# A fused cross-attention and expert block: weighted sums moved in front of the remainders and the scores in 41 of 64 steps

## The reference

```
q = layernorm(x) @ Wq;  k = ctx @ Wk;  v = ctx @ Wv
probs = softmax(q k^T / 8)          (per batch and head, 128 x 128)
x = x + tanh(g_xattn) * ((probs @ v) @ Wo + bo)
```

```
de = tokens scattered to the experts' slots by (top-2 choice, rank in arrival order)
eo = relu(de @ fc1^T + b1) @ fc2 + b2
x = x + tanh(g_ffn) * sum over the 2 choices of gate * eo
```

## Time and profile before

| | |
|---|---|
| median of 3 runs | 995.57 us (991.43 to 996.29) |
| the profiled execution | 994.87 us, span 993.1 us |
| TensorE busy | 949.4 us, 96% |
| VectorE busy | 676.3 us, 68% |
| ScalarE busy | 508.1 us, 51% |
| GpSimd busy | 281.8 us, 28% |
| mean granted clock of TensorE | 0.983 |

### The profile page before, as it was taken

How to read it: one execution, slowest core, us unless ns; L and a number is a source line. 1 busy time by engine, 2 the same in 40 slices (tenths; PEclk the granted TensorE clock), 3 DMA queues, 4 the chain that set the end, 5 groups by cost and what they waited for, 6 DMA issues and landing times.

```text
span 993.1 us, 18998 instructions
## 1 busy us (share of the span) xinstructions
PE 949.4 (96%) x7199; PEld 823.4 (83%) x7199; DVE 676.3 (68%) x1542; ACT 508.1 (51%) x1573; POOL 281.8 (28%) x293
## 2 busy tenths in 40 slices
PE   7799999999999999999999888999999999999996
PEld 5587877888878878878888786999999999999995
DVE  5768687686785886886776862757575665657572
ACT  3567376465664773673754621535444343435352
POOL 6803025024033043042041133222222223232222
PEclk8989999999999999999999998999999999999998
DMA  9096003011020021021011015254342435252521
GB/s 259 22 298 194 22 2 107 23 41 67 22 86 24 22 92 38 2 86 44 1 44 44 13 52 187 66 117 101 76 128 50 128 49 130 49 130 56 141 53 22
DMA packets 63099, 76.63 MB, mean 77 GB/s; under 512 B 6033, under 2 KB 55096, under 8 KB 63008
## 3 DMA queue, kind: packets, MB, share of 16 engines
q1 hardware_dynamic: 50720, 59.18, 20.0%
q0 software_dynamic: 12288, 16.23, 9.0%
HBM read 46.52 MB, written 29.49 MB: 77 GB/s over the span
## 4 chain that ended last, share of the span: by engine, by line
PE 73%; ACT 11%; DVE 8%; POOL 3%; DMA 2%; issue 2%; SPq 1%; POOLq 0%; DVEq 0%; another core or an unknown queue 0%
PE down L1211 6%; PE down L1210 6%; PE down L1209 6%; PE up L1195 6%; PE up L1196 6%; PE up L1197 6%; PE score L545 4%; ACT probs_odd L733 4%; ACT work L733 4%; PE out_bank L533 4%; PE probT L520 4%; DVE negmax L913 2%; PE rT L1179 2%; PE query_bank L466 2%; PE query_bank L464 2%
## 5 line engine op out<-in xcount | busy, mean ns | idle before, releaser
L1151 POOL DMA_INDIRECT out_dram<-eo,index x64 | 99.4, 1553 | 282.2 <-ACT eo L1253 250.4
L1245 ACT ACTIVATE hid<-up,b 128x512 f32<-128x512 f32 x128 | 88.3, 690 | 84.8 <-PE up L1197 84.8
L733 ACT ACTIVATE probs_odd<-score,negmax 128x128 f32<-128x128 f32 x256 | 91.3, 382 | 44.6 <-DVE negmax L913 44.6
L733 ACT ACTIVATE work<-score,negmax 128x128 f32<-128x128 f32 x256 | 91.4, 383 | 42.8 <-DVE negmax L913 42.8
L407 POOL DMA_INDIRECT disp<-packed,slots x64 | 68.8, 1075 | 133.8 <-DVE slots L904 92.4
L913 DVE TENSOR_REDUCE negmax<-score 128x4 f32<-128x512 f32 x128 | 82.0, 682 | 28.1 <-PE score L545 27.7
L698 ACT ACTIVATE k_sb<-key_bank 128x512 f32<-128x512 f32 x64 | 38.8, 606 | 112.8 <-PE key_bank L489 111.5
L1253 ACT ACTIVATE eo<-eo_raw,gate 128x256 f32<-128x256 f32 x64 | 30.9, 506 | 122.4 <-DVE eo_raw L1315 122.4
L1306 DVE TENSOR_TENSOR hid_l<-hid,hid_h 128x512 fp32r<-128x512 f32 x128 | 88.6, 693 | 4.4
L921 DVE COPY pT<-probT 128x512 f32<-128x512 f32 x128 | 82.2, 682 | 8.7 <-PE probT L520 7.4
L1315 DVE TENSOR_TENSOR eo_raw<-down,b 128x256 f32<-128x256 f32 x64 | 25.8, 423 | 86.4 <-PE down L1211 86.4
(11 more groups left out here) (253 smaller groups left out, 2788.8 us busy)
## 6 DMA issues: line engine op xcount, KB each, us to landing
rows<-disp SPq DMA_DIRECT2D x18, 516.0 KB, 5.4
w_raw<-fc1T_dram SPq DMA_DIRECT2D x9, 1024.0 KB, 8.3
w_raw<-fc_dram SPq DMA_DIRECT2D x9, 1024.0 KB, 10.9
disp<-fixed SPq DMA_DIRECT2D x1, 8256.0 KB, 33.8
rows<-x_dram SPq DMA_DIRECT2D x16, 512.0 KB, 4.3
out_dram<-rows SPq DMA_DIRECT2D x8, 512.0 KB, 3.1
c_raw<-ctxT_dram SPq DMA_DIRECT2D x8, 256.0 KB
c_raw<-ctxT_dram SPq DMA_DIRECT2D x16, 128.0 KB
```

The lines of the kernel that those rows point to most:

```text
L733: last = nc.scalar.activation(probs[w % 2][:, c, :], score[hh][:, b * P:(b + 1) * P], ACT.Exp, bias=negmax[:, w % 2, c:c + 1], accum_out=s ...
L1151: pool.indirect_dma_start(out=out_rows[:, :], out_offset=bass.IndirectOffsetOnAxis(ap=index[half][:, i:i + 1], axis=0), in_=eo[half][:, i, ...
L1245: nc.scalar.activation(hid[m % 2][:, :], up[m % 2][:, :], ACT.Relu, bias=b1[par][:, m:m + 1]).then_inc(s_hid, 1)
```

## The change

In steps without a second extra piece, TensorE's weighted sums and their wait for out_bank are issued behind V's main products (and behind the one extra piece, where there is one), in front of the two remainders and the scores. In steps with a second extra piece the order is as before.

```
             if kinds[1:]:
                 pe.wait_ge(s_at_split, w)
                 misc(kinds[1], out_bank, u // NP)
+            if w >= 0 and not kinds[1:]:
+                pe.wait_ge(s_at_split, w)
+                weigh_values(w)
             if u + 1 < STEPS:
                 keys_rest(u + 1)
             if i < STEPS:
                 values_rest(value_bank, i)
             scores(u)
-            if w >= 0:
-                if kinds[1:]:
-                    pe.wait_ge(*misc_done(kinds[1], u // NP))
-                else:
-                    pe.wait_ge(s_at_split, w)
+            if w >= 0 and kinds[1:]:
+                pe.wait_ge(*misc_done(kinds[1], u // NP))
                 weigh_values(w)
```

## The result

The changed kernel takes 1017.95 us (median of 6 runs, 1015.63 to 1021.03), the kernel before 994.83 (6 runs, 991.43 to 997.3): ratio 1.0229, 95% interval 1.0208 to 1.025. The direction was as predicted, the size not: 9.3 us were forecast, 23 came, and the time lies over the range. The profiled execution (1021.03 us, span 1019.2) is the slowest of the six, 26.1 over that of before.

The account below looks back on a forecast made before the run. TensorE's own work and the loop from one step's scores to the next q_sb were taken as nearly level bounds. Terms 7.4, 1.0, 0.9 and 0 made 9.3 us; 994.87 + 9.3 = 1004.2, range 997.5 to 1009.5.

Parts of the forecast that it names:

- The loop in j = 4 to 6: Scores to next q_sb asks 5.74 us against TensorE's 5.13 of work, so the next extra pieces each wait some 0.6.
- LT to LX: Start of j = 4's extra piece to start of j = 5's: 7.61 us instead of 7.04, +0.57.
- LX to PR: Start of j = 5's extra piece to start of j = 6's: 7.26 us instead of 6.92, +0.34.
- PR to FA: Start of j = 6's extra piece to start of j = 7's: 7.64 us instead of 7.27, +0.37 in group 1.
- Groups 1 to 6: Losses in j = 4 to 6 of these six groups together: 7.4 us.
- group 7: Last group, all three extra pieces of j = 4 to 6 but none in j = 7: estimated loss 0.9 us.
- group 0: First group, same loop in j = 5 to 7, fewer extra pieces: estimated loss 1.0 us.
- Steps j = 0 and 1: Steps without extra piece: 0.58 us won in j = 0 does not reach the end, since the maxima stand; term 0.
- Rival D: In j = 0 VectorE's idle 1.0 before the maxima goes away, seven groups gain 2.3 us: 1001.9, chance 0.12.
- Rival C: TensorE waits more, its clock falls to half speed once per group, 8 times: 18 us more, 1013, chance 0.07.
- Rivals A and B: A: moved sums fill waits, 991, chance 0.07; B: VectorE's routing sets maxima in j = 5 and 6, 999.5, 0.14.
- the unknown of one mechanism: Weighted sums to remainders, taken as 0.98 us; 0.85 or 1.19 would move the sum by -3.0 or +4.8.

Follow-up runs that it names:

- e8: Changed order, whole computation, with GpSimd's second batch of indirect DMAs issued later, behind the next group's first row statistics: 1.0141 of the kernel before.
- e7: Order before the change, whole computation, with GpSimd's second batch of indirect DMAs issued later, behind the next group's first row statistics: 0.9975 of the kernel before.
- e10: As e8, with ScalarE's copy to q_sb put in front of the second four exponentials: 997.89 us, 1.0044 of the kernel before.
- e11: As e7, with ScalarE's copy to q_sb put in front of the second four exponentials: 1002.1 us, 1.0091 of the kernel before.
- e3: Against the kernel before, the weighted sums move only in j = 1 of groups 1 to 7 (7 steps): 1.2% slower.

## Why the prediction was wrong

*The loop in j = 4 to 6* was right in its mechanism and nearly so in size. LT to LX came as 7.65 (7.61 forecast), LX to PR as 7.36 (7.26), PR to FA as 7.76 (7.64). The loop itself was exact (5.74); the sums took 1.03 up to the remainders, not 0.98, and LX 0.26, not 0.20. Groups 1 to 6 gave 9.1 instead of 7.4, group 7 1.08 instead of 0.9. In group 0 the two steps with an extra piece lost 1.4, where 1.0 was forecast; that this group came out 1.3 shorter is its start-up, which the sum left out.

*Steps j = 0 and 1, "Term: 0", is the step that failed*: 14.7 us in the profiled execution. Its reason was "it stands, because the maxima of j = 0 start at 228.69". I took an idle time of VectorE for a fixed point in time. Such idle times come and go with what GpSimd issues beside the scores: in j = 1 of group 3 the moved scores fell beside the second batch, and 1.50 became 2.71 (1.09 without it). Moving that batch takes 0.9% off the changed kernel (e8), but only 0.25% off the kernel before (e7). The same step had a second hole. It followed the loop only in j = 4 to 6, though the sums were moved out of it in j = 1 too: without the hold, O0 comes at 18.63 instead of 18.23 after j = 0's transposes (e8, e7), since T to T gains 0.48 in j = 0, and the wait for aT_l and the loop take 0.9 back. By these traces, one execution each, the 14.7 divide so: 6.3 are group 1's late x with the fall of the clock behind it, 1.3 are group 7's, and 7.0 stand in groups 2 to 6. Of these 7.0, 1.7 are the loop (e8 less e7, both without the batch) and the other 5.3 what the second batch costs more in the changed order than in the old one.

*Rival D* named the right suspect, GpSimd's indirect DMAs, with the wrong sign: I asked only what happens if the hold goes, not what happens if the scores move into another one. *Rival C* came in part: two falls of the clock instead of eight, worth some 2.2 us from O0 to O1 in group 2 and up to 2.9 in group 1 (from the sums of j = 1 to K's main products of j = 2 it takes 7.55, in e8 4.66); but behind waits of 4.15 and 3.60, not behind those of 0.5 at LX, PR and FA. *Rivals A and B* fell: LX, PR and FA wait for q_sb in every group that has them from group 1 on, and VectorE is idle before the maxima behind LX and PR.

The range was too narrow because it held the unknown of one mechanism for 23 steps and nothing for the j = 0 and 1 steps, which had an unexplained idle time in the rows.

What stays open: which path delays TensorE's signals while GpSimd issues indirect DMAs, and why it did not in j = 0 of group 2. The first batch still delays j = 0 of groups 3 to 7 in every version with the changed sums there (maxima 1.6 to 1.8 after the scores; k_sb in e8 included), and taking it away was not tried. How much group 1 loses on an average execution was not measured.

## What to carry to other kernels

When work is moved along an engine's queue, ask for each loop through other engines whether the moved piece lay inside its cover: here 1 us of sums behind the scores lay inside a loop of 5.74, and in front of them it was added to it. An idle time that the rows don't explain is a term with its own bounds, and what ends it must be found before it may be called fixed. Before judging an order, shorten the loop that it runs against: with q_sb copied 1.37 us earlier and the second batch moved, the same move gained 0.4% (e10 against e11).

## What the runs showed of the hardware

- Beside GpSimd's indirect DMAs, engines that wait for TensorE mostly start late: k_sb 1.87 instead of 0.53 after the remainders' start, maxima 2.10 to 4.25 instead of 1.09 after the scores' (j = 1 of the changed kernel). In j = 0 of group 2 they did not. Additions on GpSimd in the same place do nothing of the kind.
- The granted clock fell to 0.50 behind waits of TensorE of 4.15 and 3.60 us (after), 2.96 (e8) and 2.44 and 1.90 (e3, before O0 at 171.44 and 453.41), and stayed at 1.00 behind one of 2.06 (after, group 3).
- Beside a split of GpSimd (1.30 for 128x512), four instructions of VectorE with 16 columns took 2.47 us instead of 0.80.
- Weighted sums (column halves) to remainders (row halves) took 1.03 us, where scores to weighted sums took 0.98.
